# The low parts of the projections: VectorE in four pieces instead of GpSimd in one

## The chip, the cores and the metric

The kernel runs on one core of a Trainium2 chip. The metric is the device time of one execution in microseconds (us), as the median of several runs. Five engines work side by side on the core: TensorE (PE; its weight loads are listed apart as PEld), VectorE (DVE), ScalarE (ACT), GpSimd (POOL) and SyncE (SP), which in this kernel mostly issues DMA transfers. They wait for each other through semaphores, and each executes its own instructions strictly in order.

## The reference

```python
# x: 16 sequences x 512 rows x 256 channels; ctx: 16 x 64 x 128; 16 heads of 16 channels
def attention(x, cross_input, ...):
    q, k, v = heads(x @ Wq + bq), heads(x @ Wk + bk), heads(x @ Wv + bv)
    att = einsum('bhqd,bhkd->bhqk', q, k) * scale          # causal mask
    y = softmax(att) @ v
    qc, kc, vc = heads(x @ Wcq + bcq), heads(ctx @ Wck + bck), heads(ctx @ Wcv + bcv)
    y = y + softmax(einsum(qc, kc) * scale) @ vc           # cross attention, 64 keys
    return merge(y) @ Wp + bp
x = x + tanh(g_xattn) * attention(layernorm(x), ctx, ...)
x = x + tanh(g_ffn) * ffn(layernorm(x), ...)               # router, top 2 of 16 experts,
                                                           # a convolved shared expert
```

## The kernel before

The program has two phases. The attention phase (about 1240 us) goes through the 16 sequences one after another; the expert phase behind it does the feed-forward part. Only the attention phase is touched.

**Score products in bf16 with three parts.** The queries, cross queries, keys and cross keys of one half of the heads (`c` = 0 or 1, eight heads each) stand side by side as 1600 columns of `q32`: the column groups `COLS[0..3]` of 512, 512, 512 and 64 columns. Each fp32 value is split into three bf16 parts, high, middle and low, in `parts[:, 0]`, `parts[:, 1]` and `parts[:, 2]`. ScalarE evicts the projection of group i into `q32` (L727), makes the high part (L734) and, one group later, the middle part (L741). VectorE subtracts the high part from `q32` (`subtract_part`, L1053, written "sub i" below). The low part is `q32` minus the middle part. When all of `parts` is there (semaphore `split_done`), SyncE writes it to DRAM (`write_parts`, L399) and reads it back restacked (`read_stack`, L412 and L417) into `stack[c]`, from which TensorE multiplies the scores of the next sequence.

**The pipeline.** Iteration b of the loop (`kind` "mid"; "first" is the one without a predecessor, "last" and "post" close the loop) works on three sequences at once: the output and the routing of sequence b-1, the scores and values of b, the normalisation and the projections of b+1. It has two halves, c = 0 and c = 1. Each half begins with the four projections, with "max units" between them, and goes on with `NST` = 24 steps k = 0..23. In each step TensorE makes one score unit (L1275, into the ring of three `scalar_bank`), which ScalarE turns into exponentials (L787), and what the tables `besides(kind, c, k)` list beside it.

**The ring of VectorE's banks.** What stands beside the steps goes through three PSUM banks, `vector_bank` 0 to 2, in the order of `vector_units(kind)`: TensorE fills the next bank, VectorE empties it, and TensorE may fill a bank again only after VectorE has emptied the unit of three fills before (`claim_v`). The units that matter here are the max units u0, u1, ... (the score products once more without the low terms, L1309 and L1312 or L1305, reduced to row maxima by VectorE at L1113), the two transposes of the attention output (yT0 and yT1, L1372, copied at L1135), the transposed maxima mT (L1234, copied at L1117), and the output projection (wp0 to wp3, L1381, added at L1141). In half 0 of a mid iteration, steps 0 to 4 hold: u6; u7, yT0; yT1, mT; u8; u9, wp0.

**The low parts before.** In the prologue VectorE makes them group by group (`low_part`, L1058). In the 15 iterations that have both a current and a next sequence, GpSimd makes them with one operation over all 1600 columns (`low_parts`, L640), once per half, 30 times in all. In half 0 it stands behind the addition of the output bias (L652, four instructions) and ahead of the causal masks (`mask_group`, L628); in half 1 it stands ahead of the masks of that half.

**SyncE's order.** In either half SyncE first writes the transposed maxima to DRAM and reads them back into the stack (`max_rows`, L425 and L427, the latter after a wait for the former to land), and only then comes `write_parts`.

## Time and profile before

| | |
|---|---|
| median of 3 runs | 1699.74 us (1693.65 to 1700.99) |
| the profiled execution | 1703.96 us, span of its profile 1702.2 us |
| busy PE / DVE / ACT / POOL | 1572.1 / 1243.5 / 840.8 / 925.3 us |
| mean granted TensorE clock | 0.977 of full |
| L640 on GpSimd | 30 times, 96.7 us |
| L1058 on VectorE (prologue) | 8 times, 4.5 us |

The table is read as follows. The busy times are sums over the whole program, so they say which engine has the most work and not which one the others wait for at a given place. That is read from the timelines of single iterations. Rows of the timeline give start, duration, engine, line and operation, output and inputs, a count where like instructions are merged, and in brackets the idle time just before, with what ended it. VectorE's consecutive instructions overlap a little: a row's duration reaches past the start of the next one.

### The profile page before, as it was taken

What the parts mean: (1) busy time and instruction counts of PE and PEld (TensorE: products, weight loads), DVE (VectorE), ACT (ScalarE), POOL (GpSimd) and SP (SyncE); (2) the same over time, 40 slices, a digit from 0 to 9 for tenths busy, and PEclk for the clock granted to TensorE, in tenths of its full rate; (3) what the DMA queues carried; (4) which work ended last, traced back from release to release, by engine and by line L of the source; (5) the groups of instructions that cost most, each with busy time, mean ns of one, the idle gap of its engine ahead of it and who ended that gap; (6) DMA issues with size and microseconds to landing.
All of it is one profiled execution on the core that took longest, in us unless ns stands there. A gap on an engine that the chain in (4) does not pass through costs nothing.

```text
span 1702.2 us, 36719 instructions
## 1 busy us (share of the span) xinstructions
PE 1572.1 (92%) x11515; PEld 951.9 (56%) x11515; DVE 1243.5 (73%) x3367; ACT 840.8 (49%) x1716; POOL 925.3 (54%) x1553
## 2 busy tenths in 40 slices
PE   3898899999999999999999999999957999997997
PEld 1455455555555555555555555455535999984553
DVE  4776677787787777778777777877744866656776
ACT  3365455656565566656555665555522444431110
POOL 2245455455555455655645555464546766637775
PEclk8999899999999999999999999999978999998999
DMA  6655666546556564555465454646274666646886
GB/s 179 158 139 101 103 129 138 124 115 157 108 153 125 129 131 122 146 117 155 118 143 131 117 146 115 155 103 146 55 185 126 180 174 169 175 144 212 255 260 188
DMA packets 214951, 247.95 MB, mean 146 GB/s; under 512 B 50920, under 2 KB 168176, under 8 KB 214768
## 3 DMA queue, kind: packets, MB, share of 16 engines
q1 hardware_dynamic: 142768, 158.67, 40.2%
q10 hardware_dynamic: 54656, 51.26, 9.5%
q0 software_dynamic: 17344, 35.75, 8.1%
q8 instruction: 93, 1.52, 0.4%
q14 instruction: 90, 0.74, 0.2%
HBM read 160.04 MB, written 85.53 MB: 144 GB/s over the span
## 4 chain that ended last, share of the span: by engine, by line
PE 69%; DVE 9%; POOL 7%; issue 5%; DMA 5%; ACT 3%; SPq 1%; POOLq 0%; DVEq 0%; ACTq 0%
PE scalar_bank L1264 9%; PE pv_self L1338 9%; PE scalar_bank L1275 8%; PE vector_bank L1759 7%; POOL pt L1880 7%; PE vector_bank L1312 6%; DVE nmax L1113 4%; PE vector_bank L1309 4%; PE vector_bank L1381 4%; PE vector_bank L1221 3%; PE pv_cross L1321 3%; PE vector_bank L1254 3%; PE pv_cross L1767 2%; PE scalar_bank L1748 2%; PE pv_self L1767 2%
## 5 line engine op out<-in xcount | busy, mean ns | idle before, releaser
L1113 DVE TENSOR_REDUCE nmax<-vector_bank 128x1 f32<-128x384 f32 (+4 forms) x832 | 512.4, 640 | 107.9 <-PE vector_bank L1312 101.2
L787 ACT ACTIVATE pt<-scalar_bank 128x512 f32<-128x512 f32 x640 | 363.3, 598 | 243.9 <-PE scalar_bank L1275 241.5
L628 POOL TENSOR_SCALAR_AFFINE_SELECT pt<-pt 128x256 f32<-128x256 f32 (+1 forms) x640 | 224.1, 366 | 151.6 <-ACT pt L787 142.6
L1275 PE MATMUL scalar_bank<-stack 99*64 99x512 bf16 (+4 forms) x1280 | 295.2, 322 | 4.0 <-DMA stack<-max_scratch 3.0
L1312 PE MATMUL vector_bank<-stack 96*128 96x128 bf16 (+3 forms) x1024 | 250.2, 303 | 0.0
L1309 PE MATMUL vector_bank<-tri,ident_b 128*128 128x128 bf16 (+2 forms) x704 | 176.4, 251 | 38.9 <-DVE nmax L1113 18.0
L640 POOL TENSOR_TENSOR parts<-q,parts 128x1600 bf16<-128x1600 f32 x30 | 96.7, 3222 | 208.9 <-ACT parts L741 208.9
L1309 PEld LDWEIGHTS vector_bank<-tri,ident_b 128*128 128x128 bf16 x704 | 68.4, 97 | 214.0 <-DVE nmax L1113 117.5
L1591 POOL DMA_INDIRECT pt<-xn_rows,idx x144 | 144.6, 1004 | 78.2 <-issue 62.0
L1264 PE MATMUL scalar_bank<-xnT,w_qk 128*128 128x512 f32 x384 | 183.9, 603 | 1.1 <-ACT xnT L718 1.1
L1338 PE MATMUL pv_self<-pt,vst 128*32 128x512 f32 (+3 forms) x2048 | 181.2, 443 | 3.0 <-ACT usum L752 2.0
L583 POOL DMA_INDIRECT lists<-tokens,slot x134 | 136.1, 1015 | 38.1 <-issue 19.9
L1880 POOL DMA_INDIRECT pt<-results,rows_out x128 | 123.0, 961 | 59.1 <-issue 40.6
L1759 PE MATMUL vector_bank<-pt 128*128 128x128 f32 x1152 | 152.3, 275 | 0.1
L1275 PEld LDWEIGHTS scalar_bank<-stack 99*128 99x128 bf16 (+1 forms) x1280 | 102.7, 101 | 72.6 <-issue 23.3
L1759 PEld LDWEIGHTS vector_bank<-pt 128*128 128x128 f32 x1152 | 140.0, 192 | 0.4 <-ACT pt L1607 0.4
L727 ACT ACTIVATE q<-scalar_bank,bias 128x512 f32<-128x512 f32 (+1 forms) x128 | 75.3, 589 | 112.6 <-PE scalar_bank L1264 112.6
L1312 PEld LDWEIGHTS vector_bank<-stack 96*128 96x128 bf16 x1024 | 96.2, 99 | 46.9 <-issue 25.4
L635 POOL TENSOR_TENSOR y<-y,yc 128x256 f32<-128x256 f32 x64 | 46.3, 724 | 130.6 <-DVE y L1130 128.7
L787 ACT ACTIVATE ct<-scalar_bank 128x512 f32<-128x512 f32 x128 | 75.6, 590 | 55.2 <-PE scalar_bank L1275 52.7
L1264 PEld LDWEIGHTS scalar_bank<-xnT,w_qk 128*128 128x128 f32 x384 | 68.4, 193 | 51.7 <-issue 49.7
L1053 DVE TENSOR_TENSOR q<-q,parts 128x512 f32<-128x512 f32 (+1 forms) x128 | 76.7, 600 | 20.4 <-ACT parts L734 16.2
(215 smaller groups left out, 2679.8 us busy)
## 6 DMA issues: line engine op xcount, KB each, us to landing
qk_scratch<-parts SPq DMA_DIRECT2D x32, 1200.0 KB, 5.6
stack<-qk_scratch SPq DMA_DIRECT2D x120, 192.0 KB, 3.5
results<-pt ACTq DMA_DIRECT2D x144, 128.0 KB
stack<-qk_scratch SPq DMA_DIRECT2D x248, 72.0 KB, 3.9
stack<-qk_scratch SPq DMA_DIRECT2D x124, 128.0 KB, 3.4
stack<-qk_scratch SPq DMA_DIRECT2D x240, 36.0 KB, 3.7
xt<-in_x_dram ACTq DMA_DIRECT2D x15, 512.0 KB, 4.2
stack<-qk_scratch SPq DMA_DIRECT2D x120, 64.0 KB, 3.3
```

The source lines that it names most:

```text
L583: pool.indirect_dma_start(out=lists[:, :], out_offset=bass.IndirectOffsetOnAxis(ap=slot[:, i:i + 1], axis=0), in_=tokens[:, i % QT:i % QT ...
L628: pool.affine_select(out=v, in_=v, compare_op=ALU.is_ge, fill=0.0, base=0, pattern=pat, channel_multiplier=-1).then_inc(masked, 1)
L787: act.activation(dst, bank(kind, ("st", c, k))[:, :], ACT.Exp, scale=SCALE).then_inc(scalar_drained, 1)
L1113: dve.tensor_reduce(dst, src, axis=AX, op=ALU.max, negate=True).then_inc(vector_drained, 1)
L1264: last = pe.matmul(ps[:, :], wq[("q", "cq", "k")[i]][:, k, c, :], xnT[:, k, :], start=(k == 0), stop=(k == KC - 1))
L1275: return pe.matmul(out, stack[c][0:rows, head, key0:key0 + nk], stack[c][0:rows, head, q0:q0 + nq], start=True, stop=True, **kw)
L1309: pe.matmul(ps[:, 0:n * w].rearrange("p (h t) -> p h t", t=w)[:, :, qt * P:w], ident_b[:, :], tri[:, 0:n, :], start=True, stop=False, skip ...
L1312: last = pe.matmul(ps[:, i * w:(i + 1) * w], stack[c][0:STACK, h0 + i, qt * P:(qt + 1) * P], stack[c][0:STACK, h0 + i, K0:K0 + w], start=F ...
L1338: last = pe.matmul(pv_self[32 * j:32 * j + 32, kt * P:T], vst[:, kt, c, HEAD_GROUP * g + j, :], src, start=(kt == KT_ORDER[0]), stop=(kt = ...
L1591: pool.indirect_dma_start(out=self.xg[r], out_offset=None, in_=self.xn_rows[:, :], in_offset=bass.IndirectOffsetOnAxis(ap=self.idx[r][:, 0 ...
L1759: last = pe.matmul(psGU[q][:, m * P:(m + 1) * P], self.staged[q][:, c, m, :], self.xT[q][:, c, :], start=(c == 0), stop=(c == KC - 1))
L1880: pool.indirect_dma_start(out=self.got[b % 2][:, m, t, :], out_offset=None, in_=self.results[:, :], in_offset=bass.IndirectOffsetOnAxis(ap ...
```

## The change

GpSimd's `low_parts` goes. VectorE makes the low parts of all sequences with `low_part`, one instruction per column group: groups 0 and 1 behind sub 2 and sub 3 of the same half, groups 2 and 3 at the beginning of steps 2 and 3, ahead of what stands beside these steps.

```diff
-            def low_parts(kind, b, c):
-
-                pool.wait_ge(m_ready, 4 * SPLIT.upto(kind, b, c))
-                pool.tensor_tensor(parts[:, 2, :], q32[:, :], parts[:, 1, :], ALU.subtract).then_inc(split_done, 1)
-
             def body(kind, b):
...
-                if nxt and cur:
-                    low_parts(kind, b, 0)
                 if cur:
                     mask_group(kind, b, 0, 0)
...
-                if nxt and cur:
-                    low_parts(kind, b, 1)
                 if nxt and not cur:
                     rstd_of(2)
...
                         ln_apply(n, LN_ROWS[c, k])
+                if PARTS[kind][1] and PARTS[kind][2] and k in (2, 3):
+                    low_part(kind, b, c, k)
                 for name in besides(kind, c, k):
...
                         if nxt:
                             subtract_part(kind, b, c, i)
-                        if kind == "pro" and i > 0:
-                            low_part(kind, b, c, i - 1)
+                        if kind == "pro" and i > 0 or nxt and i in (2, 3):
+                            low_part(kind, b, c, i - 1 if kind == "pro" else i - 2)
```

The diff moves the lines behind it: L1053, L1058, L1113, L1117, L1135 and L1141 of the kernel before are L1044, L1049, L1106, L1110, L1128 and L1134 in the changed one.

VectorE, half 0 of a mid iteration, from sub 2 to wp0, before (`nmax1` rows are max units):

```order
L1053 TENSOR_TENSOR q32<-q32,parts 128x512
L1053 TENSOR_TENSOR q32<-q32,parts 128x64
L1113 TENSOR_REDUCE nmax1<-vector_bank0 128x1
L1113 TENSOR_REDUCE nmax1<-vector_bank1 128x1
L1135 COPY yT<-vector_bank2 128x512
L1135 COPY yT<-vector_bank0 128x512
L1117 COPY mT01<-vector_bank1 24x512
L1113 TENSOR_REDUCE nmax1<-vector_bank2 128x1
L1113 TENSOR_REDUCE nmax1<-vector_bank0 128x1
L1141 TENSOR_TENSOR xr<-vector_bank1,xr 128x256
```

and the same place now:

```order
L1044 TENSOR_TENSOR q32<-q32,parts 128x512
L1049 TENSOR_TENSOR parts<-q32,parts 128x512
L1044 TENSOR_TENSOR q32<-q32,parts 128x64
L1049 TENSOR_TENSOR parts<-q32,parts 128x512
L1106 TENSOR_REDUCE nmax1<-vector_bank0 128x1
L1106 TENSOR_REDUCE nmax1<-vector_bank1 128x1
L1128 COPY yT<-vector_bank2 128x512
L1049 TENSOR_TENSOR parts<-q32,parts 128x512
L1128 COPY yT<-vector_bank0 128x512
L1110 COPY mT01<-vector_bank1 24x512
L1049 TENSOR_TENSOR parts<-q32,parts 128x64
L1106 TENSOR_REDUCE nmax1<-vector_bank2 128x1
```

Two low parts now stand ahead of u6, one between yT0 and yT1, and the short one between mT and u8.

VectorE, the same steps of half 1, from sub 2 on, now (the rows without L1049 are those of before, in the same order; `logit`, `z4` belong to the routing):

```order
L1044 TENSOR_TENSOR q32<-q32,parts 128x512
L1049 TENSOR_TENSOR parts<-q32,parts 128x512
L1044 TENSOR_TENSOR q32<-q32,parts 128x64
L1049 TENSOR_TENSOR parts<-q32,parts 128x512
L1106 TENSOR_REDUCE nmax0<-vector_bank2 128x1
L960 TENSOR_TENSOR logit<-logit,m4 128x64
L1106 TENSOR_REDUCE nmax0<-vector_bank0 128x1
L1049 TENSOR_TENSOR parts<-q32,parts 128x512
L1106 TENSOR_REDUCE nmax0<-vector_bank1 128x1
L1110 COPY mT11<-vector_bank2 24x512
L964 TENSOR_REDUCE z4<-prob 128x4
L1049 TENSOR_TENSOR parts<-q32,parts 128x64
```

The third low part stands here between u7 and u8, and the short one behind the transposed maxima.

TensorE, half 0, the rows between yT0 and wp0, which the change leaves as they are:

```order
L1372 MATMUL vector_bank2<-ident,y 128x128 x4
L1275 MATMUL scalar_bank1<-stack 128x512
L1372 MATMUL vector_bank0<-ident,y 128x128 x4
L1234 MATMUL vector_bank1<-ident_b,mparts1 24x128 x4
L1275 MATMUL scalar_bank2<-stack 128x384
L1275 MATMUL scalar_bank2<-stack 128x128
L1309 MATMUL vector_bank2<-tri,ident_b 128x128
L1312 MATMUL vector_bank2<-stack 128x512
L1275 MATMUL scalar_bank0<-stack 128x512
L1309 MATMUL vector_bank0<-tri,ident_b 128x128
L1312 MATMUL vector_bank0<-stack 128x512
L1381 MATMUL vector_bank1<-w_p,yT 128x256 x2
```

Nothing moved here; the numbers show which bank each unit claims: yT1 the one of u6, u8 that of yT0, u9 that of yT1, wp0 that of mT.

## Rows read from the trace of the kernel before

**Rows 1.** The page, section 1: busy time of the engines.

```profile
PE 1572.1 (92%) x11515; PEld 951.9 (56%) x11515; DVE 1243.5 (73%) x3367; ACT 840.8 (49%) x1716; POOL 925.3 (54%) x1553
```

**Rows 2.** Windows: stretch, length, busy of each engine, TensorE clock, DMA share, GB/s.

```profile
141.04:229.00 87.96, 77.60 (x581) 41.69 (x581) 59.44 (x161) 44.96 (x87) 40.94 (x79) 0.94 0.64 112
...
380.50:1129.90 749.40, 727.55 (x5789) 402.88 (x5786) 587.62 (x1600) 447.37 (x859) 406.50 (x780) 1.00 0.55 131
```

**Rows 3.** TensorE's waits, 340 to 1180 us: total us, times, longest.

```profile
PE vector_bank L1309 <- DVE nmax L1113: 11.0, 23, 0.7
PE vector_bank L1372 <- DVE nmax L1113: 5.8, 11, 0.5
```

**Rows 4.** Timeline of GpSimd, half 0 of one iteration.

```profile
671.98 3.22 POOL L652 TENSOR_TENSOR xr<-xr,bpg 128x256 f32<-128x256 f32 x4
680.84 3.22 POOL L640 TENSOR_TENSOR parts<-q,parts 128x1600 bf16<-128x1600 f32 x1 [5.63 <-ACT parts L741]
```

**Rows 5.** Timeline of VectorE, half 0 of the same iteration.

```profile
678.15 0.69 DVE L1053 TENSOR_TENSOR q<-q,parts 128x512 f32<-128x512 f32 x1
679.16 0.23 DVE L1053 TENSOR_TENSOR q<-q,parts 128x64 f32<-128x64 f32 x1 [0.32 <-ACT parts L734]
679.30 1.15 DVE L1113 TENSOR_REDUCE nmax<-vector_bank 128x1 f32<-128x384 f32 x2
680.36 1.28 DVE L1135 COPY yT<-vector_bank 128x512 f32<-128x512 f32 x2
681.56 0.40 DVE L1117 COPY mT<-vector_bank 24x512 bf16<-24x512 bf16 x1
681.89 1.27 DVE L1113 TENSOR_REDUCE nmax<-vector_bank 128x1 f32<-128x512 f32 x2
683.32 0.42 DVE L1141 TENSOR_TENSOR xr<-vector_bank,xr 128x256 f32<-128x256 f32 x1 [0.16 <-PE vector_bank L1381]
```

**Rows 6.** Timeline of TensorE over the same steps.

```profile
679.90 0.66 PE L1372 MATMUL vector_bank<-ident,y 128*128 128x128 f32 x4 [0.53 <-DVE nmax L1113]
...
681.13 0.22 PE L1309 MATMUL vector_bank<-tri,ident_b 128*128 128x128 bf16 x1
...
681.70 0.23 PE L1309 MATMUL vector_bank<-tri,ident_b 128*128 128x128 bf16 x1
...
682.11 1.10 PE L1381 MATMUL vector_bank<-w_p,yT 128*128 128x256 f32 x4
```

**Rows 7.** Timeline of ScalarE: the middle parts of groups 1 and 2.

```profile
678.02 0.61 ACT L741 ACTIVATE parts<-q 128x512 bf16<-128x512 f32 x1
...
679.51 0.62 ACT L741 ACTIVATE parts<-q 128x512 bf16<-128x512 f32 x1
```

**Rows 8.** Timeline of SyncE's queue over the same steps.

```profile
683.39 0.71 SPq L427 DMA_DIRECT2D stack<-max_scratch  x1
684.29 0.39 SPq L399 DMA_DIRECT2D qk_scratch<-parts  x1
```

**Rows 9.** Timeline of VectorE, half 1 of that iteration.

```profile
712.12 0.69 DVE L1053 TENSOR_TENSOR q<-q,parts 128x512 f32<-128x512 f32 x1
713.13 0.23 DVE L1053 TENSOR_TENSOR q<-q,parts 128x64 f32<-128x64 f32 x1 [0.32 <-ACT parts L734]
...
714.59 1.29 DVE L1113 TENSOR_REDUCE nmax<-vector_bank 128x1 f32<-128x512 f32 x2 [0.64 <-PE vector_bank L1312]
...
717.12 0.69 DVE L1113 TENSOR_REDUCE nmax<-vector_bank 128x1 f32<-128x512 f32 x1 [0.58 <-PE vector_bank L1312]
...
722.28 0.69 DVE L906 TENSOR_TENSOR vst<-vector_bank,bv 128x512 f32<-128x512 f32 x1 [0.26 <-PE vector_bank L1221]
```

**Rows 10.** Timeline of VectorE in the prologue: low parts of 512 and 64 columns.

```profile
23.14 0.83 DVE L1058 TENSOR_TENSOR parts<-q,parts 128x512 bf16<-128x512 f32 x2
```

**Rows 11.** Timeline of VectorE: sub 0 of that iteration, beside GpSimd's L652.

```profile
673.65 0.97 DVE L1053 TENSOR_TENSOR q<-q,parts 128x512 f32<-128x512 f32 x1
```

**Rows 12.** The page, section 5: GpSimd's scatters, mean ns behind the busy time.

```profile
L583 POOL DMA_INDIRECT lists<-tokens,slot x134 | 136.1, 1015 | 38.1 <-issue 19.9
```

## The prediction

> **What bounds the kernel now.** I read the busy times of the page first. TensorE is busy 1572 of 1702 us, VectorE 1244, GpSimd 925 [rows 1]. That makes GpSimd look like the engine with room, and VectorE like the second one to fill up. Sums over the program hide stages, so I went to the windows: ten iterations of the attention phase take 749.40 us, 74.94 us each, with a granted clock of 1.00, and in them TensorE is busy 97% of the time, VectorE 78%, GpSimd 54% [rows 2]. So TensorE bounds the loop, and an edit costs only what it makes TensorE wait.
>
> The third view is the list of TensorE's waits in that stretch. Nearly all of them are for VectorE, for the release of a bank: 11.0 us ahead of L1309 and 5.8 us ahead of L1372, the latter 11 times, 0.5 us each, once per iteration [rows 3]. The reader is to see that VectorE, though idle a fifth of the time, is the last to arrive at certain places. The timelines show which. At 679.90 TensorE begins yT1 after 0.53 us of idleness, just behind the end of u6, whose bank yT1 takes [rows 5, 6]. This is the place into which the change puts the new work.
>
> **What goes.** One GpSimd instruction of 3.22 us per half [rows 4], 30 in all. It ends at 684.06. Who waits for it? SyncE's write of the parts starts at 684.29, but SyncE itself only gets free from L427 at 684.10 [rows 8]; so an earlier `split_done` lets the write start no more than 0.2 us sooner, and no sooner at all if the maxima ahead of it are late. The causal masks behind it on GpSimd start late, but none of TensorE's waits in the list is for a mask. I put the removal at 0, and the lower bound at a gain of 0.2 us per half if the write chain mattered; the rows give it no waiter.
>
> **What comes.** Per half three low parts of 512 columns and one of 64. The trace has them in the prologue: the pair takes 0.83 us, of which the short one is 0.22 [rows 10], so a long one takes 0.61 of VectorE's time until the next instruction starts. A short one takes 0.14, as sub 3 does (679.16 to 679.30) [rows 5]. Together 1.97 us per half, 3.94 per iteration. The inputs are ready: the middle parts 1 and 2 end at 678.63 and 680.13 [rows 7].
>
> **Half 0, step by step** (the iteration at 675 us; every time is the old one from the rows plus what is ahead of it) [rows 5, 6]:
> - Sub 2 starts at 678.15, so low 0 at 678.76 and sub 3 at 679.37 instead of 679.16: 0.21 later, since 0.32 us of waiting for ScalarE (and the rest of the gap) is filled. Low 1 at 679.51, u6 at 680.12 instead of 679.30: 0.82 later. The wait for the high part of the 64 columns, in which VectorE stood idle, covers just this part of the two low parts.
> - TensorE's yT1 needs the bank of u6 and was waiting for it, so it moves by the same 0.82, from 679.90 to 680.72. The stall of 0.53 becomes 1.35.
> - VectorE: a copy of 512 columns holds it for 0.60 (two from 680.36 to mT at 681.56) and ends 0.68 after its start (the two rows together last 1.28). yT0 at 680.36 becomes 681.18, then low 2 at 681.78, and yT1 starts at 682.39 and ends at 683.07, where it ended at 681.64. mT moves from 681.56 to 682.99, low 3 follows at 683.32, u8 at 683.46 instead of 681.89.
> - TensorE: u8 takes yT0's bank, free at 681.86, and would start at 681.95: no new wait. u9 takes yT1's bank: before it began at 681.70, 0.06 behind its release; now 683.13, 1.43 late. wp0 takes mT's: 682.11 was 0.15 behind 681.96, now 683.54 against 683.39, again 1.43 late.
> - VectorE's wp0 can start when TensorE has filled it, at 683.32 + 1.43 = 684.75; VectorE, with 0.60 for each of u8 and u9, is free at 684.66. From here both engines run in step, both 1.43 us late, and VectorE has no backlog left: its waits of the rest of the half stay what they were.
>
> Could TensorE get the 1.43 us back later? Only from a wait for something that did not move. From step 4 on in rows 3 all it waits for is VectorE, which moved with it, and SyncE's chain moved too: mT ends 1.43 later, so L427 ends at 685.53 and the write starts at 685.72 [rows 8]. I count nothing back. Bounds: at least the 0.82 of yT1, if yT1's own lateness met slack that the rows don't show; at most the whole 1.97.
>
> **Half 1.** Sub 2 and sub 3 stand at the same distance [rows 9], so u6 is again 0.82 late. But the next one, u7, waited 0.64 us for TensorE, and TensorE takes a bank of two units further back, for there is no yT between. About 0.2 remain. Low 2 makes it 0.8 for u8 and mT, low 3 0.93, and the wait of 0.58 at 717.12 leaves 0.35; the wait of 0.26 at 722.28 leaves about 0.1, while TensorE's claims in between had more than that in hand by the rows I walked. I take 0, with 0.1 as the upper end. What the late mT delays in the write chain is needed half an iteration later.
>
> **The sum.** 14 mid iterations by 1.43 are 20.0. The first iteration has no yT and no wp; there I have no row of such a stall and take 1.0, between 0 and 1.97. Together 21.0 us. Against the profiled execution: span 1702.2 becomes 1723.2, its time 1703.96 becomes 1725. The median lay 4.2 us below that execution, so the forecast for the median is 1699.7 + 21.0 = 1721.
>
> **An unknown on top: two engines on SBUF.** Sub 0 beside GpSimd's L652 took 0.97 us, where the same instruction otherwise takes 0.69 [rows 5, 11]; L652 runs until 675.20 in four pieces [rows 4]. Low 2 of half 0, at 681.78, now meets GpSimd's masks and scatters, which start three us sooner. The bounds are 0 (they miss each other, or VectorE is first) and 0.28 as in that row, or up to 1 us where it meets one of GpSimd's scatters, which take 1.015 us each [rows 12]; each delays yT1 and so TensorE in full, 0 to 14 us in all. I take 0 for the point, since low 0 and low 1 run in GpSimd's idle time and low 2 is one chance.
> The Trainium skill (SBUF — State Buffer, section "SBUF: two separate sides") says that VectorE instructions with two SBUF inputs and GpSimd instructions that read SBUF share a port pair under an exclusive lock, and the later one blocks wholly. The 0.97 agrees with it. By the same page the removed operation could hold up VectorE's two-input instructions for up to 3.22 us, and the four new ones are all of the lockable kind.
> A rule that speaks for the change: by the Trainium skill (GPSIMD Engine Reference, "Engine selection") two-input elementwise work belongs on VectorE, as GpSimd is about twice as slow. The rows agree on the price, 3.22 against 1.97 us. By that rule alone the change would save 1.25 us a half; by the waits of TensorE it costs.
>
> **The rivals.**
> - *The lock bites* (chance 0.13): low 2 loses 0.3 to 1 us in most iterations. 14 times that: 1725 to 1735.
> - *VectorE's whole extra work shows* (0.03): 15 x 3.94 = 59 us, 1759. Against it: the idle times of half 1.
> - *The clock falls at the longer stalls* (0.04). In the stretch 141 to 229 us an iteration took 87.96 us at a mean clock of 0.94 [rows 2]; that mean is 12% of the stretch, 10.6 us, at the lower level of 1.2 GHz instead of 2.4, and so 5.3 us lost. If each mid iteration lost a quarter of that, 1.3 us, the time would be 1739. Against it: the clock stayed at 1.00 through ten iterations with all their short stalls.
> - *The lateness is taken back or the early losses shrink* (0.14, "same"): that stretch lost 13.0 us against 74.94, of a kind that ten other iterations don't have. Should the shifted transfers avoid it, 1721 - 13 = 1708. The runs shown differ by 7 us, so losses of this kind come and go.
> - *Faster* (0.04): the parts are complete at 683.54 instead of 684.06. If that released the transfers behind the loss of 13.0 us, the gain would be 13; it decides only where TensorE's new stall stays under (13.0 - 8.5)/14 = 0.3 us per iteration, and would give 1687 with no stall at all. Against it: SyncE's order, with mT now late ahead of the write.
> - My forecast has 0.62, with a range of its own of 1713 to 1730 (0.82 to 1.97 per iteration give 1711 to 1728, the spread of runs the rest).
>
> **How the numbers follow.** A measurement of this kernel tells about 0.5%, 8.5 us, from no change. Slower by more: 0.62 + 0.13 + 0.03 + 0.04 = 0.82; within: 0.14; faster: 0.04. The range of 8 in 10 goes from 1708 (the early losses gone) to 1736 (the lock in all iterations).
>
> **What would show it.** In the profile after: an iteration of 76.4 us in place of 74.94; the wait ahead of yT1 at 1.35 us instead of 0.53, a new one of about 0.6 us ahead of L1309 two units later; no new wait of TensorE in half 1; GpSimd 97 us less busy; the write of the parts in half 0 still right behind L427. The forecast is wrong if yT1's wait stays under 1 us, if u9 waits little (then low 2 met slack), if the half-1 units stall, or if low 2 lasts 1 us.

## The result, and the profile of the changed kernel

The changed kernel takes 1721.56 us (median of 4 runs, 1720.84 to 1728.91), the kernel before in the same comparison 1696.7 us (4 runs, 1693.54 to 1700.99). The ratio is 1.0156, interval 1.0126 to 1.0187: slower by 1.6%, or 24.9 us. The forecast was 1721.0 us in a range of 1708 to 1736. The profiled execution of the changed kernel took 1721.1 us, with a span of 1719.4 us.

The page's busy times, which answer to [rows 1], look like a better balance:

```profile
PE 1576.0 (92%) x11515; PEld 954.4 (56%) x11515; DVE 1294.1 (75%) x3487; ACT 841.9 (49%) x1716; POOL 837.6 (49%) x1523
```

GpSimd lost 87.7 us and 30 instructions, VectorE gained 50.6 us and 120. TensorE, which has the same 11515 instructions, shows 4 us more busy time and a span that is 17 us longer. The loop shows where. The windows of the changed kernel, for one iteration and for ten (start and end, length, busy time of each engine, TensorE's granted clock, DMA share, GB/s), answer to [rows 2]:

```profile
454.73:531.06 76.33, 72.88 (x580) 40.33 (x580) 62.07 (x169) 44.86 (x88) 34.91 (x76) 1.00 0.55 129
...
375.04:1142.49 767.45, 731.58 (x5792) 404.95 (x5791) 621.79 (x1681) 448.57 (x861) 349.94 (x760) 1.00 0.52 128
```

An iteration takes 76.33 us instead of 74.94, 1.40 us more, and seven of those ten are within 0.02 us of it; the other three take 77.6, 77.9 and 77.6. TensorE's waits between 340 and 1200 us (engine, line, whom it waited for: total us, times, longest), which answer to [rows 3]:

```profile
PE vector_bank L1365 <- DVE nmax L1106: 14.5, 11, 1.3
PE vector_bank L1302 <- DVE nmax L1106: 10.8, 23, 0.7
PE vector_bank L1302 <- DVE yT L1128: 5.6, 11, 0.5
PE vector_bank L1356 <- DVE nmax L1106: 3.4, 12, 0.3
```

The wait ahead of yT1 (L1365, before L1372) is 1.3 us once per iteration instead of 0.5; the wait of L1302 for max units is what it was (10.8 beside 11.0); and there is one new row, L1302 for a yT copy, 0.5 us once per iteration. So the 1.40 us are two items: 0.79 and 0.50, and 0.11 that shows in no wait (some 0.09 of it lies between u8 and u9: 687.63 - 686.47 is 1.16, of which 0.50 is the wait, and it was 0.57 in [rows 6]).

The timeline of VectorE in half 0 (start, duration, line, output and input, count, idle time before), against [rows 5]. One iteration, as the forecast walked it:

```profile
683.89 0.22 DVE L1044 TENSOR_TENSOR q<-q,parts 128x64 f32<-128x64 f32 x1
684.03 0.68 DVE L1049 TENSOR_TENSOR parts<-q,parts 128x512 bf16<-128x512 f32 x1
684.63 1.15 DVE L1106 TENSOR_REDUCE nmax<-vector_bank 128x1 f32<-128x384 f32 x2
685.69 0.68 DVE L1128 COPY yT<-vector_bank 128x512 f32<-128x512 f32 x1
686.29 0.68 DVE L1049 TENSOR_TENSOR parts<-q,parts 128x512 bf16<-128x512 f32 x1
686.89 0.68 DVE L1128 COPY yT<-vector_bank 128x512 f32<-128x512 f32 x1
687.49 0.40 DVE L1110 COPY mT<-vector_bank 24x512 bf16<-24x512 bf16 x1
687.82 0.20 DVE L1049 TENSOR_TENSOR parts<-q,parts 128x64 bf16<-128x64 f32 x1
687.96 1.27 DVE L1106 TENSOR_REDUCE nmax<-vector_bank 128x1 f32<-128x512 f32 x2
```

VectorE runs without a gap from low 1 to u9. Each low part of 512 columns lasts 0.68 us and holds VectorE for 0.60. TensorE in the same steps, against [rows 6]:

```profile
685.23 0.66 PE L1365 MATMUL vector_bank<-ident,y 128*128 128x128 f32 x4 [1.32 <-DVE nmax L1106]
...
686.47 0.22 PE L1302 MATMUL vector_bank<-tri,ident_b 128*128 128x128 bf16 x1
...
687.63 0.23 PE L1302 MATMUL vector_bank<-tri,ident_b 128*128 128x128 bf16 x1 [0.50 <-DVE yT L1128]
...
688.04 1.10 PE L1374 MATMUL vector_bank<-w_p,yT 128*128 128x256 f32 x4
```

yT1 begins as u6 ends (684.63 + 0.55) after 1.32 us of idleness; u9 begins as yT1's copy ends. From yT1 to wp0 it is 2.81 us here and was 2.21.

GpSimd and SyncE, at the same place, held a surprise. The page of the changed kernel has the scatters (L583) at 1038 ns, 1015 before [rows 12]. Their timelines in this iteration, GpSimd's two rows first, SyncE's three against [rows 8]:

```profile
685.95 0.29 POOL L628 TENSOR_SCALAR_AFFINE_SELECT pt<-pt 128x128 f32<-128x128 f32 x1 [6.20 <-ACT pt L778]
686.62 1.24 POOL L583 DMA_INDIRECT lists<-tokens,slot  x1 [0.38 <-issue]
...
687.92 0.31 SPq L425 DMA_DIRECT2D max_scratch<-mT  x1
690.79 0.71 SPq L427 DMA_DIRECT2D stack<-max_scratch  x1
691.68 0.39 SPq L399 DMA_DIRECT2D qk_scratch<-parts  x1
```

The same view of the kernel before, in the iteration of [rows 8]:

```profile
681.99 0.31 SPq L425 DMA_DIRECT2D max_scratch<-mT  x1
...
684.47 1.01 POOL L583 DMA_INDIRECT lists<-tokens,slot  x1 [0.16 <-issue]
```

With L640 gone GpSimd's first scatter is issued 1.30 us ahead of L425, where before it came 2.48 us behind it. L427 waits for L425's transfer to land: that took 1.40 us before (in 13 of the 14 mid iterations 1.39 to 1.41) and 2.87 here, 2.05 to 7.90 over the 14. So the parts are written 3.8 us behind L425 instead of 2.3.

### The profile page after: what moved, and what is told of

Read it like the earlier page. It is cut to its first block, busy times and chain, and to the rows that moved or that the text cites. A ratio compares the mean times of both kernels' runs of the same rounds, so it can differ in the third digit from the quotient of the medians.

```text
span 1719.4 us, 36809 instructions
## 1 busy us (share of the span) xinstructions
PE 1576.0 (92%) x11515; PEld 954.4 (56%) x11515; DVE 1294.1 (75%) x3487; ACT 841.9 (49%) x1716; POOL 837.6 (49%) x1523
## 4 chain that ended last, share of the span: by engine, by line
PE 67%; DVE 12%; POOL 7%; DMA 5%; issue 5%; ACT 3%; SPq 1%; DVEq 0%; POOLq 0%; ACTq 0%
PE scalar_bank L1257 9%; PE pv_self L1331 9%; PE scalar_bank L1268 8%; PE vector_bank L1752 7%; POOL pt L1873 6%; PE vector_bank L1305 6%; DVE nmax L1106 5%; PE vector_bank L1302 4%; PE vector_bank L1214 3%; PE vector_bank L1374 3%; PE pv_cross L1314 3%; PE vector_bank L1247 3%; PE pv_cross L1760 2%; DVE parts L1049 2%; PE scalar_bank L1741 2%
## 5 line engine op out<-in xcount | busy, mean ns | idle before, releaser
L1106 DVE TENSOR_REDUCE nmax<-vector_bank 128x1 f32<-128x384 f32 (+4 forms) x832 | 513.0, 639 | 84.1 <-PE vector_bank L1305 77.0
L628 POOL TENSOR_SCALAR_AFFINE_SELECT pt<-pt 128x256 f32<-128x256 f32 (+1 forms) x640 | 232.2, 371 | 460.5 <-ACT pt L778 449.8
L1302 PE MATMUL vector_bank<-tri,ident_b 128*128 128x128 bf16 (+2 forms) x704 | 176.2, 250 | 35.9 <-DVE nmax L1106 13.7
L1302 PEld LDWEIGHTS vector_bank<-tri,ident_b 128*128 128x128 bf16 x704 | 68.3, 97 | 212.6 <-DVE nmax L1106 99.3
L583 POOL DMA_INDIRECT lists<-tokens,slot x134 | 139.0, 1038 | 44.1 <-issue 18.7
L1693 DVE COPY pt<-stack 128x512 f32 x144 | 62.5, 434 | 36.8 <-issue 34.7
L1044 DVE TENSOR_TENSOR q<-q,parts 128x512 f32<-128x512 f32 (+1 forms) x128 | 76.5, 598 | 10.9 <-ACT parts L725 6.7
```

The source lines that it names most:

```text
L583: pool.indirect_dma_start(out=lists[:, :], out_offset=bass.IndirectOffsetOnAxis(ap=slot[:, i:i + 1], axis=0), in_=tokens[:, i % QT:i % QT ...
L628: pool.affine_select(out=v, in_=v, compare_op=ALU.is_ge, fill=0.0, base=0, pattern=pat, channel_multiplier=-1).then_inc(masked, 1)
L1106: dve.tensor_reduce(dst, src, axis=AX, op=ALU.max, negate=True).then_inc(vector_drained, 1)
L1302: pe.matmul(ps[:, 0:n * w].rearrange("p (h t) -> p h t", t=w)[:, :, qt * P:w], ident_b[:, :], tri[:, 0:n, :], start=True, stop=False, skip ...
```

## The experiments

Each kernel was timed against the kernel before on the same chip; "iteration" is the length of a mid iteration that shows no fall of the clock, in the run's profile. The first four ran on one chip, the next four on a second, the last two on a third. On the second and third chip the kernel before takes 1790.27 us (20 runs) and 1793.6 us (23 runs) instead of 1696.55 (17 runs). Most of that lies behind the attention phase: from the last yT1 to the end the profiles show 538 to 548 us on the second and third chip and 450 to 456 us on the first. So ratios are read within a chip. Lengths of iterations are compared across chips, which holds as far as like places agree: the wait of u9 is 0.50 us on the first chip and on the second, and that of yT1 0.53.

### Only the first two low parts on VectorE

Against the kernel before: groups 0 and 1 behind sub 2 and sub 3 as in the change; GpSimd makes groups 2 and 3 in one operation of 576 columns.

```diff
+                pool.wait_ge(low_some, SPLIT.upto(kind, b, c) - 2)
                 pool.wait_ge(m_ready, 4 * SPLIT.upto(kind, b, c))
-                pool.tensor_tensor(parts[:, 2, :], q32[:, :], parts[:, 1, :], ALU.subtract).then_inc(split_done, 1)
+                pool.sem_inc(passed, 1)
+                pool.tensor_tensor(parts[:, 2, K0:ALLC], q32[:, K0:ALLC], parts[:, 1, K0:ALLC],
+                                   ALU.subtract).then_inc(split_done, 1)
...
+                if i == 1 and kind != "pro":
+                    last.then_inc(low_some, 1)
...
-                        if kind == "pro" and i > 0:
+                        if kind == "pro" and i > 0 or nxt and i in (2, 3):
...
```

> VectorE makes the low parts of groups 0 and 1 only (behind sub 2 and sub 3), GpSimd those of groups 2 and 3 in one operation of 576 columns, both in both halves. Theory (TensorE pays for the lateness of the bank it waits for, and in half 0 alone): u6 is 0.8 us late and all behind it too, so the wait ahead of yT1 is 1.3 us as in the changed kernel, but no new wait stands ahead of u9: a steady iteration of 75.7 to 75.8 us, the kernel 11 to 13 us slower than the one before. Rival (VectorE's work as such costs, wherever it stands): 2 x 1.22 us per iteration, 77.4 us and 34 us slower. Rival (GpSimd's and VectorE's collisions cost): nothing in particular for this split, and VectorE rows of low parts over 0.69 us.

Measured: 1712.45 us (1708.28 to 1716.21), ratio 1.0098, interval 1.0071 to 1.0125. The iteration is 75.75 us, 0.81 over before. Its timeline of TensorE:

```profile
681.31 0.66 PE L1378 MATMUL vector_bank<-ident,y 128*128 128x128 f32 x4 [1.32 <-DVE nmax L1119]
```

The whole wait of 1.32 us is there, and no wait ahead of u9. The two low parts of 1.2 us of work cost what of them reaches past VectorE's idle time. 14 times 0.81 is 11.3 us; the ratio gives 16.6, interval 12.0 to 21.2, so some 1 to 10 us lie outside the steady iterations.

### Only the last two low parts on VectorE

Against the kernel before: GpSimd makes groups 0 and 1 in one operation of 1024 columns as soon as their middle parts are there, VectorE groups 2 and 3 in steps 2 and 3. To keep the count of `split_done` whole, VectorE's low 3 also waits for GpSimd's operation.

```diff
-                pool.wait_ge(m_ready, 4 * SPLIT.upto(kind, b, c))
-                pool.tensor_tensor(parts[:, 2, :], q32[:, :], parts[:, 1, :], ALU.subtract).then_inc(split_done, 1)
+                pool.wait_ge(m_ready, 4 * SPLIT.upto(kind, b, c) - 2)
+                pool.tensor_tensor(parts[:, 2, 0:K0], q32[:, 0:K0], parts[:, 1, 0:K0],
+                                   ALU.subtract).then_inc(low_some, 1)
...
+                if i == 3 and kind != "pro":
+                    dve.wait_ge(low_some, SPLIT.upto(kind, b, c) - 2)
...
+                if PARTS[kind][1] and PARTS[kind][2] and k in (2, 3):
+                    low_part(kind, b, c, k)
```

> The complement: VectorE makes the low parts of groups 2 and 3 only (steps 2 and 3), GpSimd those of groups 0 and 1 in one operation of 1024 columns. Theory: u6 is as early as before, the wait ahead of yT1 0.53 us as before; yT1 is copied 0.61 late, so a wait appears ahead of u9 and moves all by about 0.6: an iteration of 75.5 to 75.6 us, 8 to 10 us slower than before; with the other split it adds up to the whole 1.40. Rival (VectorE's work as such): 2 x 0.75, 76.4 us, 21 us slower.

Measured: 1752.07 us (1746.13 to 1761.96), ratio 1.0339, interval 1.0303 to 1.0374; the iteration is 77.62 us in the one place where the clock stays and 78.2 to 78.5 in the others. Neither theory had that. The timelines of GpSimd, VectorE and TensorE in one iteration tell it:

```profile
775.70 2.12 POOL L641 TENSOR_TENSOR parts<-q,parts 128x1024 bf16<-128x1024 f32 x1 [3.50 <-ACT parts L743]
...
776.15 1.76 DVE L1055 TENSOR_TENSOR q<-q,parts 128x64 f32<-128x64 f32 x1 [0.32 <-ACT parts L736]
777.83 1.14 DVE L1120 TENSOR_REDUCE nmax<-vector_bank 128x1 f32<-128x384 f32 x2
...
778.43 0.66 PE L1379 MATMUL vector_bank<-ident,y 128*128 128x128 f32 x4 [2.06 <-DVE nmax L1120]
```

Sub 3, 64 columns that took 0.23 us in [rows 5], takes 1.76 here: it starts inside GpSimd's operation and ends as that ends, at 777.8. Behind it stands u6, and for u6 waits yT1: 2.06 us instead of 0.53. The Trainium skill (SBUF — State Buffer, section "SBUF: two separate sides") says that an instruction of VectorE with two SBUF inputs and one of GpSimd take the shared ports for their whole length, the later one blocking fully. The 1.76 us agree with it. Then the clock fell. Windows of the same kernel, 2 us each from 776.3 on, with the columns as above:

```profile
776.30:778.30 2.00, 0.07 (x1) 0.00 (x0) 2.00 (x2) 1.66 (x5) 1.53 (x1) 1.00 0.00 0
778.30:780.30 2.00, 1.83 (x12) 1.14 (x13) 2.00 (x5) 0.61 (x2) 1.06 (x2) 0.80 0.00 0
780.30:782.30 2.00, 2.00 (x7) 1.04 (x6) 2.00 (x5) 0.97 (x2) 1.81 (x3) 0.50 0.06 13
```

TensorE did next to nothing for 2 us, and then its granted clock was 0.50 of full, 1.2 GHz instead of 2.4. That happened behind 13 of the 14 stalls of 2.06 us. The one that ends at 387.69 is followed by no fall, and so its iteration of 77.62 us can be read in parts. TensorE shows there the wait of u9 too, 2.40 us behind the start of yT1:

```profile
390.09 0.23 PE L1316 MATMUL vector_bank<-tri,ident_b 128*128 128x128 bf16 x1 [0.51 <-DVE yT L1142]
```

The 2.68 us over before are 1.53 at yT1, 0.51 at u9, 0.47 ahead of mT's matmul in half 1 (L1241, 5.2 us in 11 times; sub 3 takes 1.77 us in that half too) and 0.17 net in other places. The iterations with the fall are longer by another 0.6 to 0.9 us, and there the wait of u9 is gone, since the slower TensorE comes to it later. One iteration is little to price the last two low parts by, so another kernel was made for them (below). This one shows what a meeting of two such instructions can cost.

### The change in half 1 alone

Against the changed kernel: half 0 gets GpSimd's operation back, half 1 keeps VectorE's.

```diff
+                if nxt and cur:
+                    low_parts(kind, b, 0)
...
-                if PARTS[kind][1] and PARTS[kind][2] and k in (2, 3):
+                if PARTS[kind][1] and PARTS[kind][2] and c == 1 and k in (2, 3):
...
-                        if kind == "pro" and i > 0 or nxt and i in (2, 3):
+                        if kind == "pro" and i > 0 or nxt and c == 1 and i in (2, 3):
```

> The change in half 1 only; in half 0 GpSimd's operation stands as before. Theory: half 1 hides its four instructions behind VectorE's waits for TensorE, an iteration of 74.9 to 75.0 us, no difference in time (0 to 2 us). Rival (half of the work, half of the cost): 75.6 us and 12 us slower.

Measured: 1695.64 us (12 runs, 1688.02 to 1701.85), ratio 0.999, interval 0.9969 to 1.001. The iteration is 74.95 us, and L427 follows L425 by 1.38 to 1.40 us in half 0 in all 14. VectorE takes nearly 2 us of work more per iteration and the time is the same: half 1 is free, and all of the loss comes from half 0.

### The scatters of half 0 two steps later

Against the changed kernel, to give L425's transfer its 1.4 us back. No arithmetic is left out.

```diff
-                    first = 8 if (c, g) == (1, 1) else 3
+                    first = {(1, 1): 8, (0, 0): 5}.get((c, g), 3)
```

> The changed kernel with the two scatters of half 0 behind steps 5 and 6 of the masks instead of steps 3 and 4, about where they ran in time before. In the profile after, GpSimd's first scatter comes 1.3 us ahead of SyncE's write of the transposed maxima (2.5 us behind it before), and that write takes 2.0 to 7.9 us until SyncE goes on, where it took 1.4. Theory (the scatter delays the write): the distance falls back to 1.4 us in half 0, TensorE's waits for max_scratch (7.6 us in all) shrink to those of before (3.0), the steady iteration stays at 76.34 and the time falls by 2 to 7 us against the changed kernel. Rival (the distance comes from something else, such as VectorE's low parts): it stays at 3 us, and the time too.

Measured: 1726.7 us (1722.47 to 1734.64), ratio 1.0169, interval 1.0138 to 1.02. SyncE's queue in one iteration:

```profile
694.87 0.31 SPq L425 DMA_DIRECT2D max_scratch<-mT  x1
696.27 0.71 SPq L427 DMA_DIRECT2D stack<-max_scratch  x1
697.17 0.39 SPq L399 DMA_DIRECT2D qk_scratch<-parts  x1
```

That the scatter's place delays the landing is shown: with the scatter behind L425 (695.55) it takes 1.40 us again, in 12 of 14 iterations (4.52 and 3.70 in the other two). A gain in time does not show: the iteration stays at 76.33 and the median is not below that of the changed kernel, though the two intervals overlap and would hide a gain of some 5 us. TensorE's waits for `max_scratch` went from 7.2 to 5.0 us over the attention phase, and the profiled execution, a long one with a span of 1732.9 us, lost its time in the first three mid iterations (243.5 us instead of 235.8). The expected gain of 2 to 7 us did not come.

### The last two low parts alone, without GpSimd

Against the changed kernel: the low parts of groups 0 and 1 are left out in all sequences behind the first, so `parts` keeps there the low parts of the first, and the scores have wrong low terms.

```diff
-                        if kind == "pro" and i > 0 or nxt and i in (2, 3):
-                            low_part(kind, b, c, i - 1 if kind == "pro" else i - 2)
+                        if kind == "pro" and i > 0:
+                            low_part(kind, b, c, i - 1)
```

> The changed kernel without the low parts of groups 0 and 1 (left out in the 15 iterations, so the cross-query and query columns keep stale low parts); GpSimd makes none, so nothing of GpSimd's can stand in the way of sub 3, as its 1024-column operation did in the run before (sub 3 took 1.76 us instead of 0.23 there, TensorE waited 2.06 us and fell to the lower clock in every iteration, 78.4 us each). Theory: the wait ahead of yT1 is back at 0.53, one of about 0.6 us appears ahead of u9, the iteration is 75.5 to 75.6 us, and the time 8 to 10 us above the kernel before. If the whole loss of the run before were the place of low 2 and low 3, this one would be as slow as that one.

Measured: 1800.74 us (1797.17 to 1807.65) beside 1790.27, ratio 1.0064, interval 1.0036 to 1.0092; the iteration is 75.55 us. TensorE's two rows:

```profile
677.19 0.66 PE L1365 MATMUL vector_bank<-ident,y 128*128 128x128 f32 x4 [0.53 <-DVE nmax L1106]
679.59 0.23 PE L1302 MATMUL vector_bank<-tri,ident_b 128*128 128x128 bf16 x1 [0.50 <-DVE yT L1128]
```

The wait of yT1 is that of before, that of u9 is the new one, as in the one iteration of the kernel with GpSimd's 1024 columns in which the clock stayed. 0.61 here and 0.81 for the first two low parts make 1.42, the whole change 1.40: the two places add up, and there is no third.

### The unit u6 first, in the changed kernel

u6, for which yT1 waits, is reduced ahead of sub 3, low 0 and low 1.

```diff
+                    if name[0] == "sm" and (kind, c, k) == ("mid", 0, 0):
+                        continue
...
+                        if i == 3 and (kind, c) == ("mid", 0):
+                            maxima(kind, b, 1, (SM_PRE,))
                         if nxt:
                             subtract_part(kind, b, c, i)
...
+                        if i == 3 and (kind, c) == ("mid", 0):
+                            low_part(kind, b, c, 0)
+                            low_part(kind, b, c, 1)
```

> The changed kernel with u6 drawn ahead of sub 3 and of low 0 and low 1 in half 0 (sub 2, u6, sub 3, low 0, low 1, u7). Theory: from sub 2 to u9 VectorE has no idle time left in the changed kernel, so the order within that stretch decides only where TensorE waits: the wait ahead of yT1 goes to 0, one of about 1.2 us appears ahead of mT, and yT1 is copied when it was; the iteration stays at 76.3 us, no difference from the changed kernel. Rival (the late u6 is what costs): 0.8 us per iteration come back, 75.5 us and 11 us faster than the changed kernel.

Measured: 1820.93 us (1818.9 to 1829.48) beside 1790.27, ratio 1.0187, interval 1.0151 to 1.0223; the iteration is 76.33 to 76.35 us in four of thirteen. TensorE in one of these:

```profile
690.20 0.38 PE L1234 MATMUL vector_bank<-ident_b,mparts 128*24 128x128 bf16 x4 [1.37 <-DVE nmax L1108]
691.90 0.23 PE L1309 MATMUL vector_bank<-tri,ident_b 128*128 128x128 bf16 x1 [0.50 <-DVE yT L1130]
```

The wait moved whole from yT1 to the next claim, mT's, 1.37 us for u7, and nothing was won. In eight of the other nine iterations the granted clock fell within 2.5 us behind this wait, and they take 77.7 to 78.0 us (the first 81.8); so the kernel as a whole is if anything slower than the changed one, which was not run on this chip. The lateness does not belong to one unit; it belongs to all that stands behind the low parts in VectorE's row.

### The same low parts, later in the row

Against the changed kernel, in the mid half 0: low 0 stands in step 5, low 1 in step 6, low 2 and 3 in step 7, beside the output projection, where TensorE makes four f32 matmuls per unit and VectorE waits 0.65 us at a time.

```diff
+            LOW_PLACES = {5: (0,), 6: (1,), 7: (2, 3)}
...
-                if PARTS[kind][1] and PARTS[kind][2] and k in (2, 3):
-                    low_part(kind, b, c, k)
+                if PARTS[kind][1] and PARTS[kind][2]:
+                    for i in (LOW_PLACES.get(k, ()) if (kind, c) == ("mid", 0) else {2: (2,), 3: (3,)}.get(k, ())):
+                        low_part(kind, b, c, i)
...
-                        if kind == "pro" and i > 0 or nxt and i in (2, 3):
+                        if kind == "pro" and i > 0 or nxt and i in (2, 3) and (kind, c) != ("mid", 0):
```

> The changed kernel with half 0's low parts in later steps: low 0 ahead of wp1 (step 5), low 1 at the start of step 6, low 2 and low 3 ahead of wp3 (step 7), where VectorE waited 0.65, 0.17 and 0.66 us for TensorE. Same amount of work as the changed kernel. Theory (only lateness at a bank costs): the wait ahead of yT1 is 0.53 again, none ahead of u9, an iteration of 75.0 to 75.3 us, 15 to 18 us faster than the changed kernel and 0 to 5 us slower than the one before; the write of the parts starts 3 us later and may add some waits of TensorE for the stack. Rival (VectorE's amount of work): 76.3 us.

Measured: 1795.77 us (11 runs, 1785.1 to 1801.4) beside 1790.27, ratio 1.0036, interval 1.0018 to 1.0053. The iteration is 75.07 us. VectorE in steps 5 and 6:

```profile
677.86 0.42 DVE L1137 TENSOR_TENSOR xr<-vector_bank,xr 128x256 f32<-128x256 f32 x1 [0.16 <-PE vector_bank L1377]
678.20 0.68 DVE L1049 TENSOR_TENSOR parts<-q,parts 128x512 bf16<-128x512 f32 x1
678.93 0.42 DVE L1137 TENSOR_TENSOR xr<-vector_bank,xr 128x256 f32<-128x256 f32 x1
679.27 0.68 DVE L1049 TENSOR_TENSOR parts<-q,parts 128x512 bf16<-128x512 f32 x1
```

The wait that low 0 fills is this one, in the changed kernel:

```profile
690.32 0.42 DVE L1134 TENSOR_TENSOR xr<-vector_bank,xr 128x256 f32<-128x256 f32 x1 [0.65 <-PE vector_bank L1374]
```

Low 0 takes the place of these 0.65 us. The same instructions in another place of the same half cost 0.12 us per iteration instead of 1.40. This is the strongest evidence for place against work.

### The unit u6 first, in the kernel before

Only u6 is moved ahead of sub 3; GpSimd's operation stays.

```diff
+                    if name[0] == "sm" and (kind, c, k) == ("mid", 0, 0):
+                        continue
...
+                        if i == 3 and (kind, c) == ("mid", 0):
+                            maxima(kind, b, 1, (SM_PRE,))
                         if nxt:
                             subtract_part(kind, b, c, i)
```

> The kernel before, with u6 drawn ahead of sub 3 in half 0 of the mid iterations and nothing else. Before, VectorE idles 0.32 us there for ScalarE's last high part, with u6 filled and TensorE waiting for its bank 0.53 us later. Theory: the wait ahead of yT1 is gone, VectorE runs without a gap from sub 2 to u9, and the iteration is 0.3 to 0.5 us shorter, 74.4 to 74.6 us: 4 to 7 us faster than the kernel before. Rival (the wait just moves to the next bank): 74.9 us.

Measured: 1782.03 us (median of 10 runs; the lowest 1773.06; one run of 2500.14 stands far out and is not in the ratio; the median of the other nine is 1781.33) beside 1790.27, ratio 0.9937, interval 0.9917 to 0.9957. The iteration is 74.53 us, 0.40 under before: the wait of 0.53 ahead of yT1 is gone, and 0.17 us stand ahead of mT.

It was run again on a third chip beside the next kernel:

> The kernel before with the unit u6 ahead of sub 3, run again beside e9_movedu6 on one chip, since the first time it stood in another call. Expected: iteration 74.53 to 74.54 us and 0.4 to 0.9% under the kernel before. Rival: the gain of 0.6% was of that chip's longer expert phase; then it is 0.3% or less here with the same iteration.

Measured: 1790.43 us (12 runs, 1778.57 to 1795.66) beside 1793.6 (23 runs, 1787.22 to 1809.31), ratio 0.9969, interval 0.9944 to 0.9994; the iteration is 74.53 to 74.54. Fourteen times 0.40 are 5.6 us, 0.31%, in the middle of this interval. The 0.63% on the second chip (0.50% by the medians, with the one long run left out) had something on top that did not repeat. The kernel is faster than the one before, by 0.3 to 0.6% in the two comparisons.

### Both moves together

The changed kernel with the low parts of the mid half 0 in steps 5 to 7, and u6 ahead of sub 3.

> The changed kernel with the low parts of the middle half 0 moved as in e7_moved, and the scores unit u6 issued ahead of sub 3 on VectorE as in e8_u6before. Both theories rest on one chain in half 0: VectorE's release of the vector bank (yT1). If the position on VectorE is all that costs (my theory), the two edits are independent: the iteration falls from the 75.07 us of e7_moved by the 0.40 us that the same move of u6 gave the kernel before (74.94 to 74.54), to 74.6 to 74.8, and the time is within 3 us of that of the kernel before on the same chip. Rival: the low parts cost as work wherever they stand; then the move of u6 gives nothing here, the iteration stays at 75.0 to 75.1, and the time is about 6 us over the kernel before.

Measured: 1797.54 us (12 runs, 1792.17 to 1800.49) beside 1793.6, ratio 1.0009, interval 0.9985 to 1.0032. The iteration is 74.78 us in most, 0.29 under the 75.07 without u6's move, where the same move gave the kernel before 0.40; the longest wait ahead of a later max unit is 0.9 us, where it is 0.7 in the kernel before. The timelines of GpSimd, VectorE and TensorE show where these 0.24 us come from:

```profile
683.73 0.42 POOL L628 TENSOR_SCALAR_AFFINE_SELECT pt<-pt 128x256 f32<-128x256 f32 x1
684.32 1.23 POOL L583 DMA_INDIRECT lists<-tokens,slot  x1 [0.17 <-ACT pt L778]
...
683.86 0.84 DVE L1049 TENSOR_TENSOR parts<-q,parts 128x512 bf16<-128x512 f32 x1
684.96 0.79 DVE L1049 TENSOR_TENSOR parts<-q,parts 128x512 bf16<-128x512 f32 x1
...
690.40 0.28 PE L1309 MATMUL vector_bank<-tri,ident_b 128*128 128x256 bf16 x1 [0.92 <-DVE nmax L1111]
```

Low 0 and low 1 start inside a mask and inside a scatter of GpSimd and last 0.84 and 0.79 us instead of 0.68, 0.27 us together; that is in size what the wait has more, and what the iteration has over u6's move alone. The fit is read from the rows; no run takes GpSimd's instructions away there. The time is 1.6 us over before by the ratio, and 3.9 by the medians; 14 iterations would make it 2.2 us less, so some 4 us were lost outside them, if they are more than noise (the interval of the ratio is 4 us wide to either side), of a size with what the profiles show in the first three mid iterations (241.9 us here, 224.3 for three of 74.78). So the low parts can be taken from GpSimd at no loss that this measurement tells, and without a gain: with them the iteration is 0.25 us longer than u6's move alone makes it.

## Why the prediction was right

**The time** of 1721.0 us was met to 0.6 us, and part of that is luck. The forecast counted from a median of 1699.7, which was 1696.7 in the comparison, and added 21.0, where the medians differ by 24.9 (21.4 to 31.7 by the interval of the ratio); the two misses cancel. What holds without luck is the iteration.

**The place.** Its main step, that TensorE would pay in half 0 for the lateness of VectorE's releases, is shown by four runs: half 1 alone costs nothing, the first two low parts 0.81 us per iteration, the last two 0.61, and all four in another place 0.12.

**The terms.** For yT1 it forecast a wait of 1.35 us and the trace has 1.32; for u9 about 0.6 against 0.50; for the iteration 1.43 more against 1.40. The low part was taken at 0.61 us of VectorE's time, it is 0.60. That the 0.82 and the further 0.60 would add, and not overlap, is what the sum of the two part changes shows.

**Half 1** was taken at 0, upper end 0.1 per half. The kernel with the change in half 1 alone has the iteration of before to 0.01 us.

**The removal at 0.** GpSimd got 88 us less to do, and no wait of TensorE in the steady stretch became shorter by more than 0.4 us over its 840 us. The sign named for it was 97 us: the masks (L628) are busy for 232.2 us instead of 224.1 and the scatters for 139.0 instead of 136.1.

**Nothing is given back.** So it is in the iteration. Over the whole execution the sum is less clean. 14 times 1.40 are 19.6 us; the forecast had 20.0 and 1.0 for the first iteration, and the medians differ by 24.9. The 1.0 was a guess without a row: in the profiles the yT1 of the first mid iteration starts 1.27 us later than before, 0.8 of it its own longer wait, so some 0.5 us came ahead of it. In the profiled executions mid iterations 4 to 13 take 767.47 us against 749.96, which is 17.5, 14.0 of it from the ten times 1.40; the first three take 3.8 us less than before (235.8 against 239.6), since the profiled execution of before had lost 14.8 us there, 13.0 of them in the first [rows 2], and that of after 6.8. What is left of the 24.9, about 5 us, fits the falls of the clock below: the mean granted clock is 0.972 in the middle of the changed kernel's four runs and 0.975 in that of the 17 runs of the kernel before on this chip, and 0.003 of 1720 us is an estimate of 5 us. But the four runs don't order by their clock, and with one profile of each kernel this is argued and not shown.

**The lock** had a chance of 0.13 and did not bite VectorE: the low parts of 512 columns last 0.68 to 0.69 us, all 96 of the execution. The losing side was GpSimd, whose scatter beside low 2 took 1.24 us instead of 1.01. The experiment with GpSimd's 1024 columns shows 1.53 us where the order of start falls the other way. The size set for the lock, 0.3 to 1 us, was for a meeting with L652 or a scatter. Where low parts did meet a mask and a scatter, in the kernel with both moves, they lost 0.16 and 0.11 us; so for these meetings the size was too large, and for an operation of 1024 columns too small.

**The clock** had a chance of 0.04 as a loss of 1.3 us in every iteration. It came in some. The windows of the changed kernel around one such place:

```profile
373.90:378.90 5.00, 3.65 (x26) 1.84 (x24) 4.86 (x11) 4.08 (x10) 0.74 (x2) 1.00 0.00 0
378.90:382.30 3.40, 2.90 (x10) 1.87 (x10) 2.43 (x6) 0.70 (x2) 2.48 (x4) 0.53 0.04 8
```

Behind the 1.32 us of idleness at 377 the granted clock is 0.53 for 3.4 us, near 1.2 GHz. That iteration takes 77.6 us, 1.28 more than its neighbours. The price of 1.3 us agrees, by luck, since the forecast had taken a quarter of 5.3 us for it without a reason; what did not come is "each". In the loop of the changed kernel the clock fell at 144, 157, 379, 840 and 1147 us. Of the three long iterations among the ten counted above, two are those at 379 and 840; the third has a wait of 1.48 us for `max_scratch` instead.

**What the prediction missed.** It said that the write of the parts would stay right behind L427. It does, but it counted L427 itself only 1.43 us later, "SyncE's chain moved too", with the old 1.40 us from L425 to L427. That distance became 2.05 to 7.90 us. The forecast noticed that GpSimd's masks and scatters start three us sooner, and asked only what they would do to VectorE, not what they would do to SyncE's queue. The step cost little in the end, because the stack is needed half an iteration later: TensorE's waits for `max_scratch` over the attention phase are 7.2 us instead of 3.0.

## What to carry to other kernels

Before work is moved from a half idle engine to a busier one, look for the instruction behind the new place for which the bounding engine waits: here 1.97 us of cheaper work cost 1.40 us in one half, nothing in the other, and 0.12 when it stood three to five steps later. A wait that an engine shows ahead of the new place is cover only up to its length, and what reaches past it is paid again at each bank that is handed over with no slack, until the first real gap. And when an instruction is removed, follow the queue behind it too: what starts sooner can get in front of another engine's transfer.

## What the runs showed of the hardware

- **A small write behind a scatter can land late.** L425's transfer landed in 1.39 to 1.41 us (13 of 14) where GpSimd's scatter was issued 2.5 us behind it, in 2.05 to 7.90 us where it was issued 1.3 us ahead, and in 1.38 to 1.41 us (12 of 14) when the scatter was moved back. To be ahead is not enough: with the first two low parts alone on VectorE the scatter was issued 0.14 to 0.18 us ahead in 13 of 14 iterations and the landing took 1.39 to 1.41 us, and with the last two alone it was issued 0.34 to 0.50 us ahead and the landing took 1.41 to 1.43. The few late landings without a scatter close ahead (2.11 us before, 4.52 and 3.70 with the scatters moved back) have another cause, which stays open. The Trainium skill (DMA: Bandwidth & Descriptors, section "Queues, rings and completion order") says that a transfer's semaphore write lands only after every earlier write of the same DMA engine, across its queues; the late landings agree with that, but no run here separates it from plain sharing of the engines.
- **Two inputs each, one at a time.** VectorE's 64-column subtraction took 1.76 us instead of 0.23 when it started 0.45 us into an operation of GpSimd on 1024 columns, and ended with it. Low parts of 512 columns that started inside a mask and inside a scatter took 0.84 and 0.79 us instead of 0.68, and the scatter 1.23 instead of 0.97.
- **The clock after a stall.** The granted clock fell to 0.50 within 2.6 us of yT1's start after 13 of 14 stalls of 2.06 us there; after 4 of 14 stalls of 1.32 us followed by one of 0.50 (the changed kernel; 3 of 14 with the scatters moved back); after 9 of 14 stalls of 1.37 us at mT followed by one of 0.50; after none of 14 stalls of 1.32 us alone (the first two low parts), and after none of the 14 of 0.53 before. A fall made the iteration longer by 1.28 us in the changed kernel, by 1.4 to 1.7 with u6 first, and by 0.6 to 0.9 behind the stalls of 2.06. Why it fell after some of the equal stalls and not after others the traces don't say.
- **Left open:** why moving the scatters back shows no gain; what the losses in the first three mid iterations depend on, whose size differs from profile to profile (228.2 us for the three with half 1 alone, 239.6 before, 224.8 would be without any); and why two of the three chips take 90 us longer behind the attention phase.
